# The upper parts of the last three output weights, rounded on GpSimd

## The chip, the cores and the metric

The kernel runs on one core of a Trainium2 chip. The metric is the device time of one execution in microseconds (us); three runs of the kernel before gave 1349.77, 1352.42 and 1352.82, median 1352.42. A matmul, the elementwise engines (VectorE is DVE in the profile, ScalarE is ACT, GpSimd is POOL) and the DMA queue of SyncE (SP) run side by side and wait for one another through semaphores.

## The reference

Two layers of cross attention run one after the other. Layer 0 works per batch with an attention over channels and a normalization; layer 1 is an ordinary attention with low-rank additions to its four weights:

```python
q = _lora_linear(hidden_states, Wq, Aq, Bq)      # 32 batches, 128 tokens, 1024 channels
k = _lora_linear(traces, Wk, Ak, Bk)             # 8 key heads, each for 4 query heads
v = _lora_linear(traces, Wv, Av, Bv)
scores = jnp.einsum('bhqd,bhtd->bhqt', q, k) / jnp.sqrt(jnp.asarray(HD, q.dtype))
attn = jax.nn.softmax(scores, axis=-1)
context = jnp.einsum('bhqt,bhtd->bhqd', attn, v)
out = _lora_linear(context, Wo, Ao, Bo)          # x @ Wo + 2 * (x @ Ao @ Bo)
return hidden_states + out
```

## The kernel before

All matmuls take float32 operands that are split in two: an upper part rounded to the matmul's format (fp32r), and a lower part, the float32 value less the upper part. Three matmuls (upper by upper, upper by lower, lower by upper) make one product.

Layer 0 with the key and value projections of layer 1 fills the first 415 us or so. Then one list of slots `w` sets the order of everything. Each engine's program walks through the same slots and issues its own share of each. Slots 0 to 255 (`QUERY_SLOTS = 256`) hold the query projection (`project_q`, L669), 8 slots to a pair of blocks; after them come 16 steps of 16 slots (`STEP`), one step for each pair of batches, with the output projection (`project_o`, L711). The other work of the attention is spread over the slots of both: scores (L730, with `maxima` on DVE, L1231 and L1236, and `exponents` on ACT, L981), scores a second time for the probabilities (`scores_again`, L763, one per slot, with `probabilities` on ACT, L998), and the context (L774, evacuated by ACT, L1011). `scores_again` of a slot alternates between two banks, so it waits until ACT has made the probabilities of the slot two before. The context of slots 2, 6, 10 and 14 of a step waits for them too.

The output projection of a pair of batches is a 2 by 2 product of blocks by seven products (Winograd's form of Strassen). Each product m has a combination of blocks of the context (`combine`, L1299 to L1314), split on DVE (`split_op`, L1289 upper, L1291 lower), and a combination of blocks of the weight, which is made once. GpSimd makes the three sums and one difference of weight blocks (`out_weights`, L1511, 16 instructions), the upper parts of all seven weights are rounded by ACT (`out_hi`, L891, two pieces of 128 by 1024 for each), and DVE takes the lower parts (`out_lo`, L1267, two pieces each). The tables `WO_UPPER` and `WO_LOWER` give the slot of each piece, counted from slot 256. Products 0 to 3 have theirs ahead of slot 256; those of products 4, 5 and 6 fall into slots 1 to 11 of the first step, beside its other work. The product m of the first step begins in slot 0, 2, 4, 7, 9, 11 or 13 of the step and waits for both pieces of its lower part (`wo_lo`, L681). DVE adds the finished products up in `add_out` (L1320).

The semaphore `wo_hi` counts ACT's pieces in order; `wo_mix` counts GpSimd's sums; `q_mm` counts blocks of the query projection, 64 in all. The upper parts of weights 4, 5 and 6 are written over tiles that the query projection reads, so they wait for its end, `q_mm` at 64 (L890).

Of the kernel before, what the change touches and what calls it, by code (L numbers as in the profile page):

```python
# [8 lines left out]
ALU = mybir.AluOpType  # L9
# [5 lines left out]
DMA = 16  # L15


def xattn_two_layers(nc, x, ctx_4096, Wq0, bq0, Wk0, bk0, Wv0, bv0, Wo0, bo0, gn_w, gn_b,
# [5 lines left out]
    NC = HID // P  # L24
# [11 lines left out]
    NG = B // GB  # L36
    PAIRS = B // 2
    PRODUCTS = 7
# [7 lines left out]
    with ExitStack() as ctx:  # L46
# [132 lines left out]
        def tile_at(name, place, dtype=F32):  # L179
            at[0] = place  # L180
            return sb(name, [P, GROUP, BANK], dtype)
# [3 lines left out]
        wo_raw = {0: w_blk[0], 1: w_blk[3], 2: w_sum[2], 3: w_sum[3], 4: w_blk[1], 5: w_blk[2], 6: w_sum[6]}  # L185
        hi_place = [*(w_place + i * BLOCK for i in (0, 4, 5, 6, 7)), hT_place, hT_place + BLOCK]
        lo_place = [block_place[0], block_place[3], sum_place[2], sum_place[3], block_place[1], block_place[2], sum_place[6]]
        wo = [[tile_at(f"wo{m}_{part}", place[m], F32R) for part, place in enumerate((hi_place, lo_place))]
              for m in range(PRODUCTS)]
# [17 lines left out]
        def f32(ap):  # L207
            return ap.bitcast(F32)
# [17 lines left out]
            "score_keys0", "score_keys1", *(f"again_in{i}" for i in range(4)), "rows_in0", "rows_in1", "v_in0", "v_in1", "sc_mm", "max", "neg", "exp",  # L226
            "ln", "lse", "lse_mm", "lse_hi", "lse_lo", "lse_out0", "lse_out1", "lse_out2", "lse_out3",
            "st_mm", "st_exp", "pv_mm", "c", "comb", "op_hi", "op_lo", "o_mm", "kept", "o",
            "wo_in0", "wo_in1", "wo_in2", "wo_in3", "wo_hi", "wo_lo", "wo_mix",
            "h_blk0", "h_blk1", "h_blk2", "h_blk3", "out0", "out1", "out2", "out3")}  # L230


# [10 lines left out]
        def units_of(b):  # L243
            if b == 0:
                return ()
            if b < 3:
                return (FIRST_Q + b - 1,)
            return (FIRST_Q + 2, FIRST_Q + 3) if b == 3 else (FIRST_Q + b,)
# [182 lines left out]

        WO_LOADS = {QUERY_SLOTS + w: i for i, w in enumerate((-31, -28, -23, -18))}
        WO_UPPER = {}
        for m, halves in enumerate(((-24, -23), (-11, -10), (-7, -6), (-3, -2), (1, 3), (4, 5), (7, 8))):
            for half, w in enumerate(halves):
                WO_UPPER.setdefault(QUERY_SLOTS + w, []).append((m, half))
        WO_LOWER = {}
        for m, halves in enumerate(((-18, -17), (-8, -7), (-4, -3), (-1, -1), (6, 7), (8, 9), (10, 11))):
            for half, w in enumerate(halves):
                WO_LOWER.setdefault(QUERY_SLOTS + w, []).append((m, half))  # L440

# [413 lines left out]
        def scalar_program(act):  # L855
# [25 lines left out]
            def out_hi(m, half):  # L881

                of = slice(2 * half, 2 * half + 2)
                if half == 0:
                    if m in (0, 1, 5):
                        act.wait_ge(S[f"wo_in{(0, 3, 0, 0, 0, 2)[m]}"], DMA)
                    else:
                        act.wait_ge(S["wo_mix"], {2: 3, 3: 1, 4: 2, 6: 4}[m])

                    act.wait_ge(S["q_mm"], NC * (NG - 1) + (1, 5, 6, 7, 8, 8, 8)[m])  # L890
                act.copy(wo[m][0][:, of, :], wo_raw[m][:, of, :]).then_inc(S["wo_hi"], 1)  # L891

            def begin_gram(b):
# [190 lines left out]
        def vector_program(dve):  # L1084
# [175 lines left out]
            def out_lo(m, half):  # L1260

                of = slice(2 * half, 2 * half + 2)
                if half == 0:

                    dve.wait_ge(S["wo_mix"], (1, 4, 4, 3, 2, 3, 4)[m])
                    dve.wait_ge(S["wo_hi"], 2 * (m + 1))
                dve.tensor_tensor(wo[m][1][:, of, :], wo_raw[m][:, of, :], f32(wo[m][0][:, of, :]),  # L1267
                                  ALU.subtract).then_inc(S["wo_lo"], 1)

# [158 lines left out]
            for w in range(END + 1):  # L1428
# [20 lines left out]
                for part in WO_LOWER.get(w, ()):  # L1449
                    out_lo(*part)  # L1450
# [28 lines left out]
        def gpsimd_program(pool):  # L1479

            pool.memset(lora_b3["kv"][:], 0.0)
            pool.memset(lora_a3["kv"][:], 0.0).then_inc(S["const"], 1)
            pool.memset(ident[:], 0.0).then_inc(S["const"], 1)
            pool.memset(score_bias[:], 0.0).then_inc(S["const"], 1)
            pool.wait_ge(S["const"], CONST["ident_zero"])
            pool.affine_select(out=ident[:], in_=ident[:], compare_op=ALU.not_equal, fill=1.0, base=0,
                               pattern=[[-1, P]], channel_multiplier=1).then_inc(S["const"], 1)

            mask = score_bias[:].rearrange("p (b e) -> p b e", b=H0)
            pool.wait_ge(S["const"], CONST["mask_zero"])  # L1490
            pool.affine_select(out=mask, in_=mask, compare_op=ALU.is_ge, fill=OFF_BLOCK, base=0,
                               pattern=[[-D0, H0], [0, D0]], channel_multiplier=1).then_inc(S["const"], 1)
            pool.wait_ge(S["const"], CONST["above"])
            pool.affine_select(out=mask, in_=mask, compare_op=ALU.is_ge, fill=OFF_BLOCK, base=D0 - 1,
                               pattern=[[D0, H0], [0, D0]], channel_multiplier=-1).then_inc(S["const"], 1)
            pool.memset(ones_row[:], 1.0).then_inc(S["const"], 1)
            pool.memset(minus_half[:], -0.5)
            pool.memset(ones_avg[:], 1.0 / P).then_inc(S["const"], 1)
            for m in ("q", "o"):
                pool.memset(lora_b3[m][:], 0.0)  # L1500
                pool.memset(lora_a3[m][:], 0.0).then_inc(S["const"], 1)

            def prep_rest(n):
                raw, hi, lo = prep_parts(n)
                pool.wait_ge(S["prep_hi"], n + 1)
                pool.tensor_tensor(lo, raw, f32(hi), ALU.subtract).then_inc(S["wkv_lo_pool" if n < FIRST_Q else "prep_lo"], 1)

            def out_sum(made, a, b):

                for c in range(GROUP):  # L1510
                    done = pool.tensor_tensor(made[:, c, :], a[:, c, :], b[:, c, :], ALU.subtract)  # L1511
                done.then_inc(S["wo_mix"], 1)

            def out_weights():
                b11, b12, b22, b21 = w_blk
                used = NC * (NG - 1)

                for i in range(2):
                    pool.wait_ge(S[f"wo_in{i}"], DMA)
                pool.wait_ge(S["q_mm"], used + 2)  # L1520
                out_sum(w_sum[3], b12, b11)
                pool.wait_ge(S["wo_in2"], DMA)
                pool.wait_ge(S["wo_mix"], 1)
                out_sum(b12, b22, b12)
                pool.wait_ge(S["q_mm"], used + 3)
                out_sum(w_sum[2], b22, w_sum[3])
                pool.wait_ge(S["wo_in3"], DMA)
                pool.wait_ge(S["q_mm"], used + 4)
                pool.wait_ge(S["wo_mix"], 3)
                out_sum(w_sum[6], b21, w_sum[2])  # L1530

            def power(b):
                pool.wait_ge(S["ve"], b + 1)
                pool.tensor_tensor(rstd, ve, minus_half[:], ALU.pow).then_inc(S["pow"], 1)

            def stack_lora(m):
                stack = S[f"lora_stack_{m}"]
                pool.wait_ge(S["const"], CONST[f"zero_{m}"])
                pool.wait_ge(S[f"lora_in_{m}"], LORA_IN[m])
                for q in range(3):  # L1540
                    pool.tensor_scalar(lora_a3[m][:, :, 32 * q:32 * q + R], lora_a[m][:, :, 0:R], 1.0, None,
                                       ALU.mult).then_inc(stack, 1)
                pool.tensor_scalar(lora_b[m][:], lora_b3[m][:], 1.0, None, ALU.mult).then_inc(stack, 1)
                pool.wait_ge(stack, 4)
                pool.tensor_tensor(lora_b[m][64:96, :], lora_b3[m][64:96, :], f32(lora_b[m][64:96, :]),
                                   ALU.subtract).then_inc(stack, 1)
                pool.wait_ge(stack, 5)

            for n in range(0, NC, 2):
                prep_rest(n)  # L1550
            for b in range(B):
                pool.wait_ge(S["x_hi"], b + 1)
                pool.tensor_tensor(x_lo[:], x_in[b % 2][:], f32(x_hi[:]), ALU.subtract).then_inc(S["x_lo"], 1)  # L1553
                if b and units_of(b - 1) and units_of(b - 1)[-1] < FIRST_O:
                    prep_rest(units_of(b - 1)[-1])
                if b:
                    power(b - 1)
                if b < 2:
                    stack_lora("qo"[b])
                for n in units_of(b)[:-1]:  # L1560
                    prep_rest(n)
            power(B - 1)

            pool.wait_ge(S["prep_mm"], N_UNITS)
            pool.wait_ge(S["h"], B)
            pool.memset(k_stack[LSE_ROWS, :, :, :].bitcast(F32), -1.0).then_inc(S["stack_ones"], 1)
            pool.wait_ge(S["stack_ones"], 1)
            out_weights()

        def sync_program(sp):  # L1570
# [342 lines left out]
```

## Time and profile before

| | |
|---|---|
| median of three runs | 1352.42 us |
| profiled execution | 1352.2 us |
| its span | 1350.4 us |
| granted clock of TensorE | 0.997 of full speed |
| busy PE, DVE, ACT, POOL | 98%, 69%, 61%, 12% of the span |

The profile's times are from the start of the span. Outside the span lie 1.8 us of the profiled execution. "Idle before" in a row is the time that the engine stood still ahead of that instruction, and behind the arrow stands what ended it. Step 0, the first pair of batches, runs on PE from 880.7 to about 915 us. POOL is idle from 863.4 us to the end.

### The profile page before, as it was taken

What the parts mean: (1) busy time and instruction counts of PE and PEld (TensorE: products, weight loads), DVE (VectorE), ACT (ScalarE), POOL (GpSimd) and SP (SyncE); (2) the same over time, 40 slices, a digit from 0 to 9 for tenths busy, and PEclk for the clock granted to TensorE, in tenths of its full rate; (3) what the DMA queues carried; (4) which work ended last, traced back from release to release, by engine and by line L of the source; (5) the groups of instructions that cost most, each with busy time, mean ns of one, the idle gap of its engine ahead of it and who ended that gap; (6) DMA issues with size and microseconds to landing.
All of it is one profiled execution on the core that took longest, in us unless ns stands there. A gap on an engine that the chain in (4) does not pass through costs nothing.

```text
span 1350.4 us, 23739 instructions
## 1 busy us (share of the span) xinstructions
PE 1326.5 (98%) x7135; PEld 1051.9 (78%) x7135; DVE 929.8 (69%) x2075; ACT 827.7 (61%) x2931; POOL 160.7 (12%) x129
## 2 busy tenths in 40 slices
PE   6999999999999999999999999999999999999999
PEld 4778888888888888888888888766767676766666
DVE  5666666666665777777777776586776777666666
ACT  4566666555550777777757776766566666665441
POOL 6533333222210000000000001400000000000000
PEclk9999999999999999999999999999999999999999
DMA  6455556667756888788777888989998999988872
GB/s 186 149 187 196 195 193 197 223 222 223 233 177 195 247 236 232 216 234 231 229 212 218 236 230 266 278 243 246 262 247 235 256 249 254 252 235 230 235 226 87
DMA packets 194817, 300.42 MB, mean 222 GB/s; under 512 B 26562, under 2 KB 93732, under 8 KB 194180
## 3 DMA queue, kind: packets, MB, share of 16 engines
q1 hardware_dynamic: 194692, 298.90, 76.6%
q8 instruction: 60, 0.98, 0.3%
q14 instruction: 65, 0.53, 0.1%
HBM read 213.88 MB, written 84.93 MB: 221 GB/s over the span
## 4 chain that ended last, share of the span: by engine, by line
PE 94%; DVE 2%; DMA 1%; ACT 1%; SPq 1%; issue 1%; DVEq 0%; ACTq 0%
PE bank L669 25%; PE bank L711 23%; PE bank L562 13%; PE bank L730 7%; PE bank L763 5%; PE bank L774 5%; PE bank L622 3%; PE bank L544 2%; PE bank L507 2%; PE bank L640 2%; PE bank L587 1%; PE bank L655 1%; PE bank L592 1%; PE bank L524 1%; PE bank L604 1%
## 5 line engine op out<-in xcount | busy, mean ns | idle before, releaser
L981 ACT ACTIVATE bank<-bank,negs 128x128 f32<-128x128 f32 x1024 | 347.2, 339 | 188.1 <-DVE negs L1236 187.7
L669 PE MATMUL bank<-hT,wq 128*128 128x512 f32 x1488 | 390.4, 400 | 0.0
L711 PE MATMUL bank<-wo,op 128*128 128x512 f32 x1344 | 345.7, 394 | 1.2 <-issue 1.2
L669 PEld LDWEIGHTS bank<-hT,wq 128*128 128x128 f32 x1488 | 263.9, 189 | 46.1
L711 PEld LDWEIGHTS bank<-wo,op 128*128 128x128 f32 x1344 | 249.0, 188 | 53.0 <-issue 2.4
L1231 DVE TENSOR_REDUCE maxes<-bank 128x4 f32<-128x512 f32 x256 | 175.5, 685 | 117.3 <-PE bank L730 116.9
L998 ACT ACTIVATE probT<-bank 128x512 f32<-128x512 f32 x256 | 151.2, 602 | 103.9 <-PE bank L763 101.4
L981 ACT ACTIVATION_READ_ACCUMULATOR bank<-bank,negs 128x1 f32 x1024 | 208.4, 204 | 0.0
L562 PE MATMUL bank<-wkv_hi,yT 128*128 128x512 f32 x512 | 201.5, 421 | 0.0
L730 PEld LDWEIGHTS bank<-k_stack,q_stack 96*128 96x128 f32 x1024 | 150.4, 191 | 16.3 <-issue 0.6
L730 PE MATMUL bank<-k_stack,q_stack 96*128 96x128 f32 x1024 | 147.3, 266 | 0.4 <-DMA q_stack<-q_dram 0.4
L763 PE MATMUL bank<-q_stack,k_stack 98*128 98x512 f32 x256 | 108.8, 426 | 1.7 <-ACT probT L998 1.7
L562 PEld LDWEIGHTS bank<-wkv_hi,yT 128*128 128x128 f32 x512 | 97.6, 191 | 13.8
L1553 POOL TENSOR_TENSOR x_lo<-x_in,x_hi 128x1024 fp32r<-128x1024 f32 x32 | 76.4, 2388 | 225.0 <-ACT x_hi L910 225.0
L562 PE MATMUL bank<-wkv_lo,yT 128*128 128x512 f32 x256 | 100.7, 393 | 0.0
L763 PEld LDWEIGHTS bank<-q_stack,k_stack 98*128 98x128 f32 x256 | 47.9, 187 | 66.9 <-issue 36.1
L1320 DVE TENSOR_TENSOR h_blk<-bank,h_blk 128x512 f32<-128x512 f32 x80 | 53.6, 686 | 66.5 <-PE bank L711 66.5
L868 ACT CAST yT<-bank 128x512 fp32r<-128x512 f32 x64 | 37.0, 580 | 94.2 <-PE bank L507 94.2
L1291 DVE TENSOR_TENSOR op<-c_sb,op 128x512 fp32r<-128x512 f32 x96 | 67.4, 702 | 3.3
L774 PE MATMUL bank<-probT,v_in 128*32 128x512 f32 x512 | 68.2, 604 | 1.1 <-ACT probT L998 1.0
L1236 DVE TENSOR_SCALAR negs<-maxes 128x4 f32<-128x4 f32 x256 | 44.9, 175 | 27.0
L1096 DVE TENSOR_TENSOR yT<-bank,yT 128x512 fp32r<-128x512 f32 x64 | 43.8, 685 | 24.9 <-ACT yT L868 24.9
(167 smaller groups left out, 1634.6 us busy)
## 6 DMA issues: line engine op xcount, KB each, us to landing
q_stack<-q_dram SPq DMA_DIRECT2D x256, 256.0 KB, 4.0
q_dram<-q_part SPq DMA_DIRECT2D x64, 512.0 KB, 4.2
q_stack<-q_dram SPq DMA_DIRECT2D x256, 128.0 KB, 4.3
y_in<-in_ctx SPq DMA_DIRECT2D x32, 512.0 KB, 4.4
x_in<-in_x SPq DMA_DIRECT2D x32, 512.0 KB, 5.2
h_dram<-h_out SPq DMA_DIRECT2D x32, 512.0 KB, 2.6
h_in<-h_dram SPq DMA_DIRECT2D x32, 512.0 KB, 3.7
k_stack<-k_dram SPq DMA_DIRECT2D x128, 128.0 KB, 3.4
```

What stands on the lines that cost most here:

```text
L562: m = pe.matmul(bank(2), yT[b % 2][:, c, part, :], w[:, c, :], start=first, stop=c == NC - 1 and part == 1)
L669: m = pe.matmul(bank(u % 2).rearrange("p (a n) -> p a n", a=2), wq[:, block, part, c, :], hT[(group + 1) % 2][:, :, of, c, :], start=c == ...
L711: mm = pe.matmul(out_bank(pair, m), op[m][:, of, c, :], wo[m][w][:, c, :], start=c == 0 and of == 0 and w == 0, stop=c == GROUP - 1 and of ...
L730: m = pe.matmul(score_bank(n)[:, j * P:(j + 1) * P], q_stack[place // GQ][SCORE_ROWS, g, j, :], k_stack[SCORE_ROWS, k % 2, g, :], start=Tr ...
L763: pe.matmul(again_bank(n), k_stack[STACK_ROWS, 2 + k % 2, g, :], again_stack(k)[STACK_ROWS, g, :, :].rearrange("p j n -> p (j n)"), start= ...
L774: m = pe.matmul(bank(3)[g * HD:(g + 1) * HD, :], v_in[:, k % 2, g, :], probT[:, (GQ * k + g) % PROBS, :], start=True, stop=True)
L981: act.activation(part, part, ACT.Exp, bias=negs[:, n % RING, j:j + 1], scale=SCORE1, accum_out=sums[:, score_column(k), g, j:j + 1]).then_ ...
L998: act.activation(probT[:, n % PROBS, :], again_bank(n), ACT.Exp, scale=SCORE1).then_inc(S["st_exp"], 1)
L1231: dve.tensor_reduce(largest, score_bank(n).rearrange("p (j t) -> p j t", j=GROUP), AX_X, ALU.max).then_inc(S["max"], 1)
L1291: dve.tensor_tensor(op_part(m, 1), tile, f32(op_part(m, 0)), ALU.subtract).then_inc(S["op_lo"], 1)
L1320: dve.tensor_tensor(block[:], *terms, ALU.add).then_inc(S["o"], 1)
L1553: pool.tensor_tensor(x_lo[:], x_in[b % 2][:], f32(x_hi[:]), ALU.subtract).then_inc(S["x_lo"], 1)
```

## The change

ACT no longer rounds the upper parts of weights 4, 5 and 6. GpSimd does, in six instructions behind its differences of blocks, once `q_mm` stands at 64; they count on a semaphore of their own, `wo_hi_pool`. The lower parts of the three weights stay on DVE, and their slots move: weight 4 from slots 6 and 7 to 4 and 5, weight 5 from 8 and 9 to 7 and 8, weight 6 from 10 and 11 to 9 and 10.

```diff
-        for m, halves in enumerate(((-24, -23), (-11, -10), (-7, -6), (-3, -2), (1, 3), (4, 5), (7, 8))):
+        for m, halves in enumerate(((-24, -23), (-11, -10), (-7, -6), (-3, -2))):
             for half, w in enumerate(halves):
                 WO_UPPER.setdefault(QUERY_SLOTS + w, []).append((m, half))
         WO_LOWER = {}
-        for m, halves in enumerate(((-18, -17), (-8, -7), (-4, -3), (-1, -1), (6, 7), (8, 9), (10, 11))):
+        for m, halves in enumerate(((-18, -17), (-8, -7), (-4, -3), (-1, -1), (4, 5), (7, 8), (9, 10))):
...
-                    dve.wait_ge(S["wo_hi"], 2 * (m + 1))
+                    dve.wait_ge(S["wo_hi"] if m < 4 else S["wo_hi_pool"], 2 * (m % 4 + 1))
...
                 out_sum(w_sum[6], b21, w_sum[2])
+
+                pool.wait_ge(S["q_mm"], NC * NG)
+                pool.wait_ge(S["wo_mix"], 4)
+                for m in range(4, PRODUCTS):
+                    for half in range(2):
+                        of = slice(2 * half, 2 * half + 2)
+                        pool.tensor_scalar(wo[m][0][:, of, :], wo_raw[m][:, of, :], 1.0, None,
+                                           ALU.mult).then_inc(S["wo_hi_pool"], 1)
```

GpSimd's queue at its end, behind the sums of blocks (`w_sum`, `w_blk`); `wo_0_142`, `wo_0_144` and `wo_0_146` are the upper parts of weights 4, 5 and 6:

```order
 L1511 TENSOR_TENSOR w_sum_131<-w_blk_128,w_blk_127 128x512 x4
 L1511 TENSOR_TENSOR w_blk_128<-w_blk_129,w_blk_128 128x512 x4
 L1511 TENSOR_TENSOR w_sum_132<-w_blk_129,w_sum_131 128x512 x4
 L1511 TENSOR_TENSOR w_sum_133<-w_blk_130,w_sum_132 128x512 x4
-L1868 UNCONDITIONAL_BRANCH
+L1537 TENSOR_SCALAR wo_0_142<-w_blk_128 128x1024 x2
+L1537 TENSOR_SCALAR wo_0_144<-w_blk_129 128x1024 x2
+L1537 TENSOR_SCALAR wo_0_146<-w_sum_133 128x1024 x2
```

The six new instructions are the last of that engine's program.

DVE in slots 5 to 9 of step 0; `wo_1_143`, `wo_1_145` and `wo_1_147` are the lower parts of weights 4, 5 and 6, `op_118` a part of the context's split, `maxes` and `negs` the maxima of the scores:

```order
+L1267 TENSOR_TENSOR wo_1_143<-w_blk_128,wo_0_142 128x1024
 L1289 TENSOR_SCALAR op_118<-c_sb 128x512
 L1291 TENSOR_TENSOR op_118<-c_sb,op_118 128x512
-L1267 TENSOR_TENSOR wo_1_143<-w_blk_128,wo_0_142 128x1024
 L1320 TENSOR_TENSOR s_sb<-bank,c_sb 128x512
 L1320 TENSOR_TENSOR h_blk_154<-s_sb,h_blk_154 128x512
 L1231 TENSOR_REDUCE maxes<-bank 128x4
 L1236 TENSOR_SCALAR negs<-maxes 128x4
-L1267 TENSOR_TENSOR wo_1_143<-w_blk_128,wo_0_142 128x1024
 L1267 TENSOR_TENSOR wo_1_145<-w_blk_129,wo_0_144 128x1024 x2
+L1267 TENSOR_TENSOR wo_1_147<-w_sum_133,wo_0_146 128x1024
 L1320 TENSOR_TENSOR h_blk_157<-bank,h_blk_157 128x512
```

Both pieces of weight 4 now stand ahead of the maxima of slot 7, and the first piece of weight 6 stands ahead of the maxima of slot 10. The number of DVE's instructions is the same.

ACT in slots 1 to 8 of step 0, the part of its queue that loses six roundings (`CAST`), as it stands before:

```order
L891 CAST wo_0_142<-w_blk_128 128x1024
L981 ACTIVATE bank,sums<-bank,negs 128x128 x4
L998 ACTIVATE probT<-bank 128x512
L1017 COPY c_sb<-bank 128x512
L998 ACTIVATE probT<-bank 128x512
L1011 COPY c_sb<-bank 128x512
L891 CAST wo_0_142<-w_blk_128 128x1024
L998 ACTIVATE probT<-bank 128x512
L891 CAST wo_0_144<-w_blk_129 128x1024
L998 ACTIVATE probT<-bank 128x512
L891 CAST wo_0_144<-w_blk_129 128x1024
```

In the changed kernel the same rows follow one another without the `CAST` rows.

## Rows read from the trace of the kernel before

**Rows 1.** Windows: busy us of PE, PEld, DVE, ACT, POOL; clock, DMA share, GB/s.

```profile
880.00:913.00 33.00, 29.63 (x148) 20.18 (x146) 30.71 (x49) 22.94 (x69) 0.00 (x0) 1.00 0.87 243
913.00:1340.00 427.00, 426.29 (x2101) 298.88 (x2098) 290.15 (x525) 239.73 (x683) 0.00 (x0) 1.00 0.87 235
```

**Rows 2.** Timeline of PE, step 0: start us, us long, instruction [idle before <- releaser].

```profile
889.34 0.51 PE L763 MATMUL bank<-q_stack,k_stack 98*128 98x512 f32 x1 [0.63 <-ACT probT L998]
...
893.80 0.51 PE L763 MATMUL bank<-q_stack,k_stack 98*128 98x512 f32 x1 [0.52 <-ACT probT L998]
...
895.33 1.06 PE L774 MATMUL bank<-probT,v_in 128*32 128x512 f32 x8 [1.02 <-ACT probT L998]
...
901.72 1.62 PE L711 MATMUL bank<-wo,op 128*128 128x512 f32 x6 [1.19 <-issue]
...
909.67 0.40 PE L763 MATMUL bank<-q_stack,k_stack 98*128 98x512 f32 x1
```

**Rows 3.** Timeline of ACT, step 0.

```profile
892.20 1.05 ACT L891 CAST wo<-w_blk 128x1024 fp32r<-128x1024 f32 x1
893.15 0.59 ACT L998 ACTIVATE probT<-bank 128x512 f32<-128x512 f32 x1
...
907.06 0.34 ACT L981 ACTIVATE bank<-bank,negs 128x128 f32<-128x128 f32 x1 [2.62 <-DVE negs L1236]
908.45 0.61 ACT L998 ACTIVATE probT<-bank 128x512 f32<-128x512 f32 x1
```

**Rows 4.** Timeline of DVE, end of the query projection and step 0.

```profile
882.39 0.68 DVE L1218 TENSOR_SCALAR q_part<-bank 128x512 fp32r<-128x512 f32 x1
...
889.89 0.69 DVE L1320 TENSOR_TENSOR h_blk<-c_sb,h_blk 128x512 f32<-128x512 f32 x1 [0.85 <-ACT c_sb L1017]
...
900.40 3.49 DVE L1267 TENSOR_TENSOR wo<-w_blk,wo 128x1024 fp32r<-128x1024 f32 x3
...
906.06 0.68 DVE L1231 TENSOR_REDUCE maxes<-bank 128x4 f32<-128x512 f32 x1
...
914.97 0.69 DVE L1320 TENSOR_TENSOR h_blk<-bank,h_blk 128x512 f32<-128x512 f32 x1 [2.15 <-PE bank L711]
```

**Rows 5.** Timeline of POOL, part of its sums of blocks.

```profile
852.63 5.02 POOL L1511 TENSOR_TENSOR w_sum<-w_blk,w_sum 128x512 f32<-128x512 f32 x4
...
857.82 5.60 POOL L1511 TENSOR_TENSOR w_sum<-w_blk,w_sum 128x512 f32<-128x512 f32 x4 [0.17 <-POOL w_sum L1511]
859.19 4.23 POOL L1511 TENSOR_TENSOR w_sum<-w_blk,w_sum 128x512 f32<-128x512 f32 x3
```

**Rows 6.** Timeline of DVE beside them.

```profile
855.27 1.15 DVE L1236 TENSOR_SCALAR negs<-maxes 128x4 f32<-128x4 f32 x1
...
858.11 1.67 DVE L1291 TENSOR_TENSOR op<-c_sb,op 128x512 fp32r<-128x512 f32 x1
```

**Rows 7.** Timeline of POOL, its two earlier roundings of 128 by 1024.

```profile
28.15 2.77 POOL L1543 TENSOR_SCALAR lora_b_q<-lora_b_q 128x1024 fp32r<-128x1024 f32 x1
...
41.47 2.78 POOL L1543 TENSOR_SCALAR lora_b_o<-lora_b_o 128x1024 fp32r<-128x1024 f32 x1
```

**Rows 8.** Timeline of DVE beside these two.

```profile
28.11 1.16 DVE L1174 TENSOR_SCALAR att<-att,att_stat 128x128 f32<-128x128 f32 x1
29.19 0.68 DVE L1096 TENSOR_TENSOR yT<-bank,yT 128x512 fp32r<-128x512 f32 x1
...
42.25 0.35 DVE L1174 TENSOR_SCALAR att<-att,att_stat 128x128 f32<-128x128 f32 x1
```

**Rows 9.** Groups by line: duration ns min/median/max; the last one busy us, mean ns, idle.

```profile
L1174 DVE TENSOR_SCALAR att<-att,att_stat x32: 285/287/1161, 28.1 to 391.4; 128x128 f32<-128x128 f32 x32
...
L1236 DVE TENSOR_SCALAR negs<-maxes x256: 169/170/1151, 438.7 to 1213.0; 128x4 f32<-128x4 f32 x128
...
L1267 DVE TENSOR_TENSOR wo<-w_blk,wo x8: 1212/1218/1226, 843.5 to 902.7; 128x1024 fp32r<-128x1024 f32 x8
...
L1291 DVE TENSOR_TENSOR op<-c_sb,op 128x512 fp32r<-128x512 f32 x96 | 67.4, 702 | 3.3
```

More of the change, by code:

```diff
@@ L228, in xattn_two_layers @@
             "st_mm", "st_exp", "pv_mm", "c", "comb", "op_hi", "op_lo", "o_mm", "kept", "o",
-            "wo_in0", "wo_in1", "wo_in2", "wo_in3", "wo_hi", "wo_lo", "wo_mix",
+            "wo_in0", "wo_in1", "wo_in2", "wo_in3", "wo_hi", "wo_hi_pool", "wo_lo", "wo_mix",
             "h_blk0", "h_blk1", "h_blk2", "h_blk3", "out0", "out1", "out2", "out3")}
@@ L884, in out_hi @@
                 if half == 0:
-                    if m in (0, 1, 5):
-                        act.wait_ge(S[f"wo_in{(0, 3, 0, 0, 0, 2)[m]}"], DMA)
-                    else:
-                        act.wait_ge(S["wo_mix"], {2: 3, 3: 1, 4: 2, 6: 4}[m])
-                    act.wait_ge(S["q_mm"], NC * (NG - 1) + (1, 5, 6, 7, 8, 8, 8)[m])
+                    if m < 2:
+                        act.wait_ge(S[f"wo_in{(0, 3)[m]}"], DMA)
+                    else:
+                        act.wait_ge(S["wo_mix"], {2: 3, 3: 1}[m])
+                    act.wait_ge(S["q_mm"], NC * (NG - 1) + (1, 5, 6, 7)[m])
                 act.copy(wo[m][0][:, of, :], wo_raw[m][:, of, :]).then_inc(S["wo_hi"], 1)
```

## The prediction

> **What bounds the kernel now.** I read the table of windows first, since the change touches one stage only. Behind step 0 PE has next to nothing to win: from 913 to 1340 us it stands still for 0.7 us, with DVE busy for 290 of 427 us [rows 1]. The stretch from 880 to 913 us is unlike it: PE is busy for 29.6 of 33 us, DVE for 30.7 [rows 1]. So in step 0 DVE sets the pace and PE follows it; behind it PE sets the pace, and whatever PE is late by at the end of step 0 is late by in the end, since no later idle time of PE can take it up.
>
> The reader should next see in PE's timeline where its 3.4 us of idle time are: 0.63, 0.52 and 1.02 us for probabilities from ACT, and 1.19 us ahead of product 4 [rows 2]. That last one has no releaser in the profile; DVE's three lower pieces began at 900.40 and the first of them, the second of weight 4, was done about 1.2 us later, at 901.6, just ahead of PE's start at 901.72 [rows 2, 4]. So it is the weight. ACT's timeline shows one cause of the others: a rounding of 1.05 us stood at 892.20 ahead of probabilities that PE wanted, done at 893.74 for PE's start at 893.80 [rows 2, 3]. At the far end of step 0 the probabilities of slot 10 (908.45 + 0.61 = 909.06) are ready 0.6 us before the scores of slot 12 begin at 909.67 [rows 2, 3]: that is PE's slack against DVE there, because the exponents ahead of them wait for DVE again, for 2.62 us [rows 3].
>
> **What goes from ACT.** Six roundings of 1.05 us, 6.3 us [rows 3]. ACT is busy for 22.9 of 33 us there [rows 1] and mostly waits for DVE, so only those ahead of wanted probabilities count: PE could win 0.52 + 1.02, and with the earlier lower part of weight 4 another 1.19, together 2.7 us, if nothing else held it. It does not keep them. After the roundings are gone the probabilities of slot 5 still stand behind the exponents of slot 5, and these behind DVE's maxima. I take this gain as passed on to the next wait for DVE, so at 0, and carry the 2.7 as a bound.
>
> **What moves on DVE.** It has the same instructions, without a pause between them in this stretch but for 0.85 us at 889 [rows 4]. A lower piece takes 1.14 us from one start to the next ((3.49 - 1.22) / 2, for three in a row with 1.22 as the length of the last [rows 4, 9]). Four pieces stood ahead of the maxima of slot 10 at 906.06 [rows 4], now five do. The maxima come 1.1 us later, and so do exponents and probabilities of slot 10; less PE's slack of 0.6 us that is +0.5 us for PE. The maxima of slots 5 and 7 are late by the same 1.1 us, but behind them PE has the room of the waits that go (2.7 us). All pieces are done by the maxima of slot 13 as before, so the order costs nothing further.
>
> **What comes to POOL.** Six instructions of the form of L1543, 2.77 us each [rows 7], 16.6 us from the end of the query projection at 880.7. The two pieces of weight 4 are there at about 887, those of weight 5 by 893 and of weight 6 by 899 even with some waiting; DVE asks for them at 893, 901 and 903 or later. So DVE never waits for the semaphore. It costs nothing as long as POOL isn't held up by more than some 4 us.
>
> **What POOL's instructions do to DVE's.** This is the term that decides. In the sums of blocks a DVE instruction that reads two SBUF tiles, or a rounding or scaling from SBUF to SBUF, stands until POOL's running instruction ends. The four of 852.63 take 1.25 us each, so one ends at 856.4: DVE's negation, 0.17 us long by itself [rows 9], began at 855.27 and lasted 1.15, to 856.42. POOL's of 857.82 ends at 859.1 (the next is recorded at 859.19): DVE's lower part, 0.70 by itself [rows 9], began at 858.11 and lasted 1.67, to 859.78 [rows 5, 6]. A subtraction with one operand from PSUM passed beside POOL's rounding in 0.68 us (L1096 at 29.19 [rows 8]). In step 0 nearly all of DVE's work is of the kind that stands still.
>
> What a rounding of 128 by 1024 on POOL holds, two instances show. L1174 takes 0.287 us, and once 1.16, once 0.35 [rows 8, 9]. The first ended at 29.27, so it began in truth at 28.98, 0.83 us behind POOL's start at 28.15. The second ended at 42.60, so at 42.31, 0.84 us behind POOL's start at 41.47. In both POOL lasted for 2.77 or 2.78 us [rows 7, 8]. I read this as: POOL's rounding keeps such DVE work out for its first 0.84 us and not for all of its 2.77. The bounds for one of them are 0 us (as the second, which lost 0.06) and 2.77 us (if it holds as the sums do).
>
> Six times 0.84 would be 5.0 us. Laid along DVE's queue from 880.7, with POOL starting as soon as its last is done and DVE's running instruction is over, the six starts meet: the second lower piece of weight 3, with the seam between two instructions (0.87 us lost), the first combination (0.25, since the two roundings of `q_part` from PSUM at 882.39 [rows 4] cover the rest), then the lower part of product 2 (0.82), the upper of 3 (0.87), the upper of 4 (0.87) and the lower of 5 (0.76): 4.4 us. About 0.2 of it goes into DVE's idle 0.85 ahead of 889.89 [rows 4].
>
> The sum for PE: 4.4 - 0.2 for the holds, + 1.1 for the order, - 0.6 for the slack = +4.7 us. The profiled execution took 1352.2 us, so 1356.9; it lay 0.2 below the median of the runs, so 1357.1 us. If POOL's rounding also keeps DVE's roundings out while it writes, it is up to 0.7 us more by the same laying out; with a second hold of 0.84 us in every piece against all kinds, 4 to 5 more, 1362.
>
> The Trainium skill ("SBUF — State Buffer", section "Who interferes with whom") says that a DVE instruction in a 2-port mode and GpSimd lock each other out, and that "whoever issues first gets the shared pair for the whole instruction". The sums of blocks agree; L1174 at 42.25 does not, for it was through 1.65 us before POOL's rounding ended. By the rule the result would be that of the first rival.
>
> **The rivals.** *The whole instruction is held.* For it speaks that the sums hold to their end [rows 5, 6]; against it the second L1174 [rows 8], though one short instruction is thin evidence. Six pieces of 2.77 are 16.6 us, less 2.1 in which DVE has three PSUM reads to do (0.7 each, as L1218 and L1231 in [rows 4]) and less 0.7 at the seams: 13.8 us lost, + 1.1 - 0.6 = +14.3, or 1366.7 us.
>
> *Nothing is held that matters* (not slower). POOL's rounding reads one tile, and no row shows DVE's two-input subtraction beside one; most of step 0's work may pass. Then the order remains, +0.5 us, 1352.9. Against it stands the first L1174.
>
> *ACT's relief decides* (not slower). Where DVE is not held and its new order doesn't reach PE, PE keeps the waits that go, 0.52 + 1.02 + 1.19 = 2.7 us [rows 2]: 1349.7. It decides only if the maxima of slots 5, 7 and 10 come no more than 0.6 us later than before. DVE's dense queue speaks against it. Even this whole gain is 0.2%.
>
> **Chances.** A partial hold 0.60, nothing held 0.20, all held 0.15, relief 0.05. Within 0.3%, which is what a measurement of this kernel can tell from no change, lies 1348.4 to 1356.5 us. The partial hold, itself 1354 to 1362, is above that in about 7 of 10 cases. So slower by over 0.3%: 0.42 + 0.15 = 0.57; within: 0.18 + 0.20 + 0.02 = 0.40; faster: 0.03. The range from 1351.8 to 1362 us takes in the partial hold and the case without any, and leaves out the full hold and the relief.
>
> **What would show it.** In the changed kernel's profile: six POOL roundings of 2.8 to 3.5 us from 880.7 or 881.3; six DVE instructions in step 0 drawn out to some 0.8 us more than their kind, each ending a fixed 0.84 us behind a start of POOL plus its own length; busy DVE from 880 to 913 near 33 us; no wait of PE ahead of product 4 by the weight; DVE's wait for product 6, which ends at 914.97 [rows 4], ending at about 919.7; the stretches behind it as before. If the drawn-out ones reach 2.5 us and end where POOL's end, the first rival is right; if none is drawn out, the second. A wait of DVE at L1267 for POOL would show my pace of POOL wrong.

## The result, and the profile after

The changed kernel takes 1355.7 us (median of 8 runs, 1354.72 to 1357.05) against 1352.05 us for the kernel before (8 runs): 1.003 times as long, 95% interval 1.002 to 1.004. The prediction was 1357.1 us, and slower by over 0.3% the likeliest case. The median lies 3.65 us above, 0.27%, so just inside the band around no change; the interval, 2.7 to 5.4 us, does not settle on which side of 0.3% the change lies. The profiled execution took 1354.72 us.

A finer measure than the time is the length of step 0 in the profile, from the start of its first output product to the start of the last half of product 6. Before it was 880.66 to 913.39, 32.7 us. Windows of the changed kernel, columns as in [rows 1]:

```profile
864.00:877.00 13.00, 13.00 (x68) 8.98 (x67) 7.70 (x12) 10.53 (x28) 0.00 (x0) 1.00 0.99 275
878.00:916.00 38.00, 31.47 (x149) 21.28 (x148) 34.42 (x48) 18.40 (x67) 17.68 (x6) 0.96 0.78 215
917.00:1340.00 423.00, 422.29 (x2081) 295.45 (x2080) 287.97 (x521) 238.08 (x676) 0.00 (x0) 1.00 0.89 236
```

Ahead of step 0 and behind it PE stands still for 0.7 us in all, as in [rows 1]; within it, for 6.5 of 38. The timeline of PE there:

```profile
878.08 1.54 PE L711 MATMUL bank<-wo,op 128*128 128x512 f32 x6
...
889.13 0.50 PE L763 MATMUL bank<-q_stack,k_stack 98*128 98x512 f32 x1 [3.02 <-ACT probT L998]
889.47 2.69 PE L711 MATMUL bank<-wo,op 128*128 128x512 f32 x6
...
896.94 1.61 PE L711 MATMUL bank<-wo,op 128*128 128x512 f32 x6 [0.24 <-DVE h_blk L1320]
900.82 0.50 PE L763 MATMUL bank<-q_stack,k_stack 98*128 98x512 f32 x1 [2.27 <-ACT probT L998]
...
905.31 0.50 PE L763 MATMUL bank<-q_stack,k_stack 98*128 98x512 f32 x1 [1.00 <-ACT probT L998]
...
911.91 0.46 PE L763 MATMUL bank<-q_stack,k_stack 98*128 98x512 f32 x1
...
915.71 1.55 PE L711 MATMUL bank<-wo,op 128*128 128x512 f32 x6
```

Step 0 lasts from 878.08 to 915.71, 37.6 us: 4.9 us more. The waits of [rows 2] are other ones now: 0.63 has become 3.02, the pair in slots 5 and 6 is gone, 2.27 and 1.00 stand in slots 7 and 9, and nothing waits ahead of product 4. That this step began 2.6 us earlier than before is no gain of the change: over the thirteen profiles of this study it began between 877.4 and 881.1 us, and two executions of the changed kernel differ in it by 1.6 us.

The timeline of DVE after, the rows that are longer than their kind, with some of their neighbours (compare [rows 4] and [rows 9]):

```profile
877.52 3.20 DVE L1267 TENSOR_TENSOR wo<-w_sum,wo 128x1024 fp32r<-128x1024 f32 x2
...
881.97 0.97 DVE L1299 TENSOR_TENSOR c_sb<-c_sb 128x512 f32<-128x512 f32 x1
...
883.77 0.64 DVE L1289 TENSOR_SCALAR op<-s_sb 128x512 fp32r<-128x512 f32 x1
884.44 1.40 DVE L1291 TENSOR_TENSOR op<-s_sb,op 128x512 fp32r<-128x512 f32 x1
...
886.55 0.50 DVE L1236 TENSOR_SCALAR negs<-maxes 128x4 f32<-128x4 f32 x1
886.63 0.68 DVE L1310 TENSOR_TENSOR c_sb<-c_sb 128x512 f32<-128x512 f32 x1
887.35 1.14 DVE L1289 TENSOR_SCALAR op<-c_sb 128x512 fp32r<-128x512 f32 x1
...
889.97 1.52 DVE L1320 TENSOR_TENSOR h_blk<-c_sb,h_blk 128x512 f32<-128x512 f32 x1 [0.75 <-ACT c_sb L1017]
...
893.19 1.14 DVE L1289 TENSOR_SCALAR op<-c_sb 128x512 fp32r<-128x512 f32 x1
```

And of POOL:

```profile
878.10 11.85 POOL L1537 TENSOR_SCALAR wo<-w_blk 128x1024 fp32r<-128x1024 f32 x4 [16.71 <-PE bank L669]
889.91 5.87 POOL L1537 TENSOR_SCALAR wo<-w_sum 128x1024 fp32r<-128x1024 f32 x2
```

The six roundings take 2.8 to 3.3 us each and are done at 895.8, before DVE asks for the last of them at 905.4. The DVE rows, each less the length of its kind before (2.36, 0.68, 0.43, 0.69, 0.43, 0.69, 0.43), exceed it by 0.84, 0.29, 0.21, 0.71, 0.71, 0.83 and 0.71: 4.3 us. The negation at 886.55 is 0.33 longer, but the next instruction began at once and is not, so that costs nothing.

### The profile page after: what moved, and what is told of

The parts are those of the page before. It is cut to its first block, busy times and chain, and to the rows that moved or that the text cites. A ratio compares the mean times of both kernels' runs of the same rounds, so it can differ in the third digit from the quotient of the medians.

```text
span 1352.8 us, 23737 instructions
## 1 busy us (share of the span) xinstructions
PE 1326.9 (98%) x7135; PEld 1051.6 (78%) x7135; DVE 933.6 (69%) x2075; ACT 823.2 (61%) x2925; POOL 178.3 (13%) x135
## 4 chain that ended last, share of the span: by engine, by line
PE 94%; DVE 3%; ACT 1%; issue 1%; DMA 1%; SPq 0%; DVEq 0%; ACTq 0%
PE bank L669 25%; PE bank L711 22%; PE bank L562 13%; PE bank L730 7%; PE bank L763 5%; PE bank L774 5%; PE bank L622 3%; PE bank L507 2%; PE bank L544 2%; PE bank L640 2%; PE bank L587 1%; PE bank L655 1%; PE bank L592 1%; PE bank L524 1%; PE bank L604 1%
## 5 line engine op out<-in xcount | busy, mean ns | idle before, releaser
L711 PE MATMUL bank<-wo,op 128*128 128x512 f32 x1344 | 346.5, 395 | 0.2 <-DVE h_blk L1320 0.2
L711 PEld LDWEIGHTS bank<-wo,op 128*128 128x128 f32 x1344 | 249.7, 189 | 51.8 <-issue 1.2
L763 PE MATMUL bank<-q_stack,k_stack 98*128 98x512 f32 x256 | 109.2, 428 | 6.9 <-ACT probT L998 6.9
L763 PEld LDWEIGHTS bank<-q_stack,k_stack 98*128 98x128 f32 x256 | 48.1, 188 | 73.2 <-issue 38.8
L1511 POOL TENSOR_TENSOR w_sum<-w_blk,w_blk 128x512 f32<-128x512 f32 x4 | 5.0, 1292 | 425.5 <-DMA w_blk<-wo_dram 425.5
```

Source lines behind the costliest of these rows:

```text
L711: mm = pe.matmul(out_bank(pair, m), op[m][:, of, c, :], wo[m][w][:, c, :], start=c == 0 and of == 0 and w == 0, stop=c == GROUP - 1 and of ...
L763: pe.matmul(again_bank(n), k_stack[STACK_ROWS, 2 + k % 2, g, :], again_stack(k)[STACK_ROWS, g, :, :].rearrange("p j n -> p (j n)"), start= ...
```

## The experiments

"Step 0" is the measure above, 32.7 us in the kernel before and 37.6 in the changed one. The ratios are to the kernel before, on the same chip.

**The new order alone.** The kernel before with

```diff
-(-1, -1), (6, 7), (8, 9), (10, 11))):
+(-1, -1), (4, 5), (7, 8), (9, 10))):
```

> The kernel before with only the lower pieces moved to their new slots; the upper parts stay on ScalarE. Theory (GpSimd's roundings hold VectorE up for 0.84 us each, and the new order costs a little): from the first product of step 0 to its last (32.7 us before, 37.6 us in the changed kernel) it takes 33.2 to 34.4 us, and the whole kernel 0.5 to 1.7 us more than before. Rival (the new order is the cause of the loss): 36 us or more, and 3.5 us more in all. Rival (ScalarE's relief is what counts, the order helps): shorter than 32.7 us.

Step 0 took 34.3 us (879.82 to 914.11), 1.6 more; the time was 1.0017 of before, 1.0008 to 1.0027. The order is not the cause of the loss, though it is a part of it. In PE's timeline the waits of slots 3, 5 and 6 stay word for word, the 1.19 ahead of product 4 is gone, and three take its place further on:

```profile
898.36 0.50 PE L763 MATMUL bank<-q_stack,k_stack 98*128 98x512 f32 x1 [0.54 <-ACT probT L998]
902.85 0.50 PE L763 MATMUL bank<-q_stack,k_stack 98*128 98x512 f32 x1 [1.02 <-ACT probT L998]
910.27 0.50 PE L763 MATMUL bank<-q_stack,k_stack 98*128 98x512 f32 x1 [0.66 <-ACT probT L998]
```

They are the maxima that stand behind the earlier lower pieces. This run holds more than the order, though: with ScalarE still rounding, DVE now asked for weight 6 before ScalarE had it, and stood still for 0.76 us, ahead of the maxima of slot 10:

```profile
903.84 1.23 DVE L1267 TENSOR_TENSOR wo<-w_sum,wo 128x1024 fp32r<-128x1024 f32 x1 [0.76 <-ACT wo L891]
```

The changed kernel has no such wait. So 1.6 us is too much for the order by itself; the next two runs give it without ScalarE's roundings.

**GpSimd's roundings alone.** The changed kernel with the old `WO_LOWER`.

> The changed kernel with the lower pieces in their old slots: GpSimd rounds, nothing else moves. Theory of the hold: step 0 takes 36.5 to 37.3 us (4.3 us of held VectorE work less at most 0.5 us of slack), the kernel some 4 us more than before; VectorE shows the same six drawn-out instructions. Rival (the new order is the cause): about 32.7 us, no change.

Step 0 took 37.0 us (880.35 to 917.37), 4.3 more; the time was 1.0031 of before, 1.0019 to 1.0042. The loss is there without the new order. GpSimd's roundings alone bring 4.3 of the 4.9 us, the order 0.6 on top.

**No roundings at all.** The six `pool.tensor_scalar` of the changed kernel taken out, and

```diff
+        for m in range(4, PRODUCTS):
+            wo[m][0] = wo[m - 3][0]
```

> The changed kernel, new order, with the six roundings of GpSimd left out: products 4, 5 and 6 use the upper parts of weights 1, 2 and 3, so this part of the result is another one. ScalarE has its relief, GpSimd nothing to do in step 0. Theory of the hold: step 0 takes 33.2 to 33.8 us (0.5 to 0.9 over before, from the order), no wait of TensorE over 1.5 us, and no fall of its clock. Rival (nothing is held, the loss is the order with ScalarE's queue): still about 37 us. Rival (the relief of ScalarE is worth 2.7 us): about 30 us.

Step 0 took 33.65 us, 0.9 more than before and 4.0 less than the changed kernel. The time was 1.0012 of before (1.0002 to 1.0022). No DVE instruction in it is drawn out. So the order costs 0.9 us without ScalarE's roundings, and GpSimd's roundings 4.0 us. One thing expected did not hold: TensorE waited for over 2 us once, and its clock did fall. Some 0.3 of the 0.9 us can be put down to that fall, by an estimate: the probabilities of slot 10 were ready at 909.13, and PE began the scores of slot 12 at 909.56, 0.43 us later, where in the changed kernel it was 0.08 (911.83 and 911.91). That leaves 0.6 for the order, as in the comparison above.

**The old order without the late roundings.**

> The kernel before with the six late roundings of ScalarE left out and nothing in their place: products 4 to 6 use the upper parts of weights 1 to 3, so this part of the result is another one. Theory (VectorE sets the pace of step 0, ScalarE's relief is passed on to the next wait): step 0 takes 32.5 to 33.0 us, as before, with the waits of 0.52 and 1.02 us for probabilities in slots 5 and 6 gone and new ones of the same sum in slots 7 to 9. Rival (the relief is worth what these waits are): 30 to 31.3 us.

Step 0 took 32.75 us, the same as before to 0.02; the time was 1.0005 (0.9994 to 1.0016). PE's timeline (line numbers are two higher, L765 is the old L763, L713 the old L711):

```profile
888.61 0.50 PE L765 MATMUL bank<-q_stack,k_stack 98*128 98x512 f32 x1 [0.64 <-ACT probT L1000]
897.33 0.50 PE L765 MATMUL bank<-q_stack,k_stack 98*128 98x512 f32 x1 [1.31 <-ACT probT L1000]
901.01 1.63 PE L713 MATMUL bank<-wo,op 128*128 128x512 f32 x6 [1.54 <-issue]
```

The 0.52 and 1.02 us of slots 5 and 6 are gone, and 1.31 in slot 7 and 0.35 more ahead of product 4 have come: 1.54 given up, 1.66 taken. In the old order relieving ScalarE is worth nothing. In the new order it is worth 0.6 us (34.3 against 33.65), for there DVE's wait of 0.76 us for ScalarE goes with it. That wait came with the new order, so it is no gain over the kernel before.

**Roundings timed to harmless work.** The changed kernel, old order, each rounding behind a wait of its own for a count that DVE reaches:

```diff
+                pace = iter((("wo_lo", 8), ("op_lo", 3), ("op_lo", 4), ("op_lo", 6), ("wo_lo", 9), ("wo_lo", 12)))
```

> The changed kernel with the lower pieces in their old slots, and each of GpSimd's six roundings waits for the VectorE instruction ahead of one that reads PSUM or of an idle time, so that its first 0.84 us fall beside work that can't be held. Theory (only the first 0.84 us are held): step 0 takes 33.2 to 34.2 us, and the six held instructions lose under 1.2 us together. Rival (a rounding holds for all of its 2.8 us): 42 us or more. Rival (a hold at its start and one at its end while it writes, each 0.84 us against all of VectorE's work): 35 us or more.

DVE's held work was 1.1 us in all (0.28, 0.17, 0.45 and 0.24), as expected: the same six instructions on GpSimd, at other moments, cost DVE a quarter. That excludes a hold of 2.8 us. Yet step 0 took 35.5 us, more than any figure of the theory; the rival with two full holds, 35 us or more, has the figure, but not the rows, which show 1.1 us held in all. The median of twelve executions was 1352.44 us (1.001 of before, 1.000 to 1.002). The profiled one was the longest, 1357.2 us, and not by step 0 alone: far behind it PE waited once for a DMA, which has nothing to do with the roundings:

```profile
1194.94 0.47 PE L763 MATMUL bank<-q_stack,k_stack 98*128 98x512 f32 x1 [1.61 <-DMA q_stack<-lse_dram]
```

Windows of step 0 in which PE was late:

```profile
904.00:906.00 2.00, 2.00 (x9) 1.64 (x8) 2.00 (x3) 1.19 (x4) 0.35 (x1) 0.63 0.86 220
906.00:908.00 2.00, 2.00 (x7) 1.71 (x7) 1.97 (x5) 0.43 (x1) 2.00 (x1) 0.51 0.69 190
908.00:909.00 1.00, 1.00 (x7) 0.35 (x10) 0.89 (x3) 0.26 (x1) 0.42 (x1) 1.00 0.80 252
```

The granted clock, the third value from the end, was at 0.5 of full speed (the 1.2 GHz level) for some 3.4 us. PE had stood still for 1.75 us ahead of 899.48 and for 1.81 ahead of 903.40.

> The paced kernel once more, for a second profile. In the first, step 0 took 35.5 us against 33.2 to 34.2 expected, with VectorE's held work at the 1.2 us expected and TensorE's clock below full from 904 to 910 us. Theory (the excess is the clock, which fell after two idle times of TensorE of 1.8 us): with the same fall step 0 takes 35.5 us again, without it 33.3 to 34.0. Rival (the excess is VectorE or ScalarE): 35.5 us also where the clock stays full.

The second profile: step 0 took 33.95 us, with the clock down again, but from 898 to about 901, right behind an idle time of 1.77 us:

```profile
898.00:899.00 1.00, 1.00 (x4) 0.82 (x3) 0.87 (x2) 0.45 (x1) 1.00 (x1) 0.50 0.79 176
899.00:901.00 2.00, 2.00 (x5) 1.02 (x4) 1.89 (x4) 0.41 (x3) 1.53 (x1) 0.50 0.94 269
```

In this one PE then still waited 0.43 us for the weight ahead of product 4, so the slow stretch was over before PE was the late one. The theory as it was put is half wrong: the clock fell and the time was short all the same. PE's rows from the start of product 4 to that of product 5, in the first profile and in the second, show where the 1.6 us between them lie:

```profile
903.40 1.91 PE L711 MATMUL bank<-wo,op 128*128 128x512 f32 x6 [1.81 <-issue]
...
909.93 1.54 PE L711 MATMUL bank<-wo,op 128*128 128x512 f32 x6
```

```profile
901.45 1.63 PE L711 MATMUL bank<-wo,op 128*128 128x512 f32 x6 [0.43 <-issue]
...
906.41 1.55 PE L711 MATMUL bank<-wo,op 128*128 128x512 f32 x6
```

This stretch took 6.53 us in the first, with the clock down and no wait in it, and 4.96 in the second, at full clock. What stands ahead of it in step 0 took 22.28 and 22.27 us, what stands behind it 6.70 and 6.72. So the whole 1.6 us are the clock's, in a stretch where PE waited for nobody. The fall costs nothing where PE would have waited for DVE next anyway, as in the second.

**Two inputs on GpSimd.**

```diff
-                        pool.tensor_scalar(wo[m][0][:, of, :], wo_raw[m][:, of, :], 1.0, None,
-                                           ALU.mult).then_inc(S["wo_hi_pool"], 1)
+                        pool.tensor_tensor(wo[m][0][:, of, :], wo_raw[m][:, of, :], wo_raw[m][:, of, :],
+                                           ALU.add).then_inc(S["wo_hi_pool"], 1)
```

> The changed kernel with GpSimd making the upper parts of weights 4 to 6 by adding the tile to itself (two inputs) in place of scaling it by one, so these parts and what comes of them are doubled in part. Theory (a two-input instruction on GpSimd holds VectorE's work to its end, 2.4 us; the scaling does so for its first 0.84 us only): step 0 takes 44 to 46 us, the kernel some 12 us more than before, and VectorE's held instructions end where GpSimd's end. Rival (each GpSimd instruction costs VectorE the same 0.84 us whatever its form): 36 to 38 us.

Step 0 took 41.05 us (877.40 to 918.45), 8.3 more than before; the time was 1.0054 of before (1.0037 to 1.007). Each instruction is shorter on GpSimd, 2.38 us, and costs far more. DVE beside them:

```profile
876.84 4.06 DVE L1267 TENSOR_TENSOR wo<-w_sum,wo 128x1024 fp32r<-128x1024 f32 x2
...
883.31 2.20 DVE L1307 TENSOR_TENSOR s_sb<-c_sb 128x512 f32<-128x512 f32 x1
885.54 2.00 DVE L1289 TENSOR_SCALAR op<-s_sb 128x512 fp32r<-128x512 f32 x1
887.57 2.26 DVE L1291 TENSOR_TENSOR op<-s_sb,op 128x512 fp32r<-128x512 f32 x1
```

The rival of one price for every form of instruction is out. The figure of 44 to 46 was too high: it let GpSimd wait for the whole of each DVE instruction between two of its own, but GpSimd's first four took 9.85 us, 2.46 each, so it lost under 0.1 us to each, and all six were through after 14.2 us.

**Half the size.** Twelve roundings of 128 by 512 in place of six.

> The changed kernel with each of GpSimd's roundings in two of 128 by 512. Theory (the hold is the time in which the input is read, one column after another, so 0.42 us for 512): step 0 takes 35.5 to 37.5 us, as the changed kernel or a little less, with twelve short delays on VectorE. Rival (0.84 us for every instruction): 40 us or more. Rival (held to the end): 46 us or more.

Step 0 took 36.1 us (1.0019 of before, 1.0008 to 1.0029), 3.3 more. DVE shows delays of about 0.3 us (0.97 for a kind of 0.69, 0.71 for 0.43), at most 0.41, and 2.7 us in all, in place of 4.3. So the hold is not a fixed price of an instruction: with half the columns it is half as long or less.

**Both engines by themselves.** The kernel before with trials behind its end; in the first two

```diff
+                    last = pool.tensor_scalar(probT[:, 0:2, :], c_sb[:, 0:2, :], 1.0, None, ALU.mult)
```

> The kernel before with six trials behind its end, some 20 us more, that touch no result: in each GpSimd runs one instruction of 128 by 1024 (scaling in trials 1 and 2, a two-input subtraction in 3 and 4, a fill in 5 and 6) and VectorE beside it twelve instructions of 128 by 128, two-input ones in the odd trials and scalings from SBUF to SBUF in the even ones. Theory: beside GpSimd's scaling VectorE's two-input instructions stand still once, for its first 0.84 us, and pass freely after; its scalings stand still there and a second time of at most 0.9 us near the end, while GpSimd writes (as the 0.50 us of a negation at 902.0 in the paced kernel suggests); beside the subtraction both stand still until its end at 2.4 us; beside the fill only the scalings are held. Rival: the scaling holds in several stretches of 0.3 us or more over its 2.8 us, for two-input work too.

Timelines of POOL (all six trials: scaling, subtraction and fill, each beside two-input work of DVE and then beside its scalings) and of DVE (from trials 1 to 3):

```profile
1345.39 2.88 POOL L1597 TENSOR_SCALAR probT<-c_sb 128x1024 f32<-128x1024 f32 x1 [484.82 <-DVE wo L1490]
1348.72 3.13 POOL L1597 TENSOR_SCALAR probT<-c_sb 128x1024 f32<-128x1024 f32 x1 [0.45 <-DVE wo L1495]
1352.36 2.34 POOL L1599 TENSOR_TENSOR probT<-c_sb 128x1024 f32<-128x1024 f32 x1 [0.51 <-DVE wo L1490]
1356.88 3.61 POOL L1599 TENSOR_TENSOR probT<-c_sb 128x1024 f32<-128x1024 f32 x1 [2.18 <-DVE wo L1495]
1360.97 0.96 POOL L1601 MEMSET probT<- 128x1024 f32 x1 [0.48 <-DVE wo L1490]
1363.33 2.32 POOL L1601 MEMSET probT<- 128x1024 f32 x1 [1.40 <-DVE wo L1495]
```

```profile
1345.55 1.12 DVE L1488 TENSOR_TENSOR wo<-wo,wo 128x128 fp32r<-128x128 f32 x1
1346.60 0.28 DVE L1490 TENSOR_TENSOR wo<-wo,wo 128x128 fp32r<-128x128 f32 x1
...
1348.82 1.06 DVE L1493 TENSOR_SCALAR wo<-wo 128x128 fp32r<-128x128 f32 x1
1349.80 0.21 DVE L1495 TENSOR_SCALAR wo<-wo 128x128 fp32r<-128x128 f32 x1
...
1352.41 2.44 DVE L1490 TENSOR_TENSOR wo<-wo,wo 128x128 fp32r<-128x128 f32 x1
```

Beside the scaling at 1345.39 one two-input instruction stood still and ended at 1346.67, so it began at 1346.39, 1.0 us behind POOL's start; the eight behind it passed in 0.28 us each while POOL worked on until 1348.27. A DVE scaling beside the next one did the same (begun in truth at 1349.67, 0.95 behind POOL's start), and those behind it passed. Beside the two-input subtraction at 1352.36 DVE's instruction ended at 1354.85, just behind POOL's end at 1354.70. Beside the subtraction at 1356.88 and beside the fill at 1363.33 DVE's scalings were not held, at 0.21 and 0.22 us each; GpSimd's instruction was, 3.61 us in place of 2.34 and 2.32 in place of 0.96: the opposite of what was expected of both. Beside the fill at 1360.97 DVE's two-input instructions went on at 0.28 us. The Trainium skill ("SBUF — State Buffer", section "Who interferes with whom") lets two SBUF inputs of DVE contend only with a GpSimd instruction that reads SBUF: by that fill, the trials agree. By its lock for a whole instruction the scaling would have held DVE for 2.9 us; the trials disagree, with 1.0. The end of POOL's scaling had no DVE scaling beside it in the trial, so the second hold wasn't tried there; that it exists rests on two rows of the changed kernel. The negation of 0.50 us at 886.55 ended at 887.05; less its own 0.17 it began in truth at 886.88, 0.15 us ahead of the end of POOL's third rounding at 887.03. The rounding of 0.64 us at 883.77, less its own 0.43, began in truth at 883.98, again 0.15 ahead of the end of POOL's second at 884.13.

**A better order for the kernel before.** Three additions and two splits of DVE stand later in step 0, behind maxima and lower pieces:

```diff
+                    sums_at = ({6: (3,), 7: (4,), 10: (5, 6), 11: (7, 8, 9), 13: (10,)} if pair == 0 else
+                               {6: (3, 4), 9: (5, 6), 11: (7, 8, 9), 13: (10,)})
...
-                    if i == 5:
+                    if i == (8 if pair == 0 else 5):
                         split_op(pair + 1, 0)
-                    if i == 9:
+                    if i == (11 if pair == 0 else 9):
                         split_op(pair + 1, 1)
```

> The kernel before with four of VectorE's works of step 0 (one sum, two additions to blocks, two splits for the next pair) moved behind the maxima and lower pieces that TensorE waits for; ScalarE rounds as before. Theory (VectorE's order sets step 0): step 0 takes 31.4 to 32.4 us, 0.3 to 1.2 less than before, and the wait of 1.19 us ahead of product 4 is gone; in the time of the kernel that is at most 0.1%. Rival (another engine sets the pace): 32.7 us.

Step 0 took 31.5 us, 1.2 less, and the wait of 1.19 is gone; the time was 0.9993 of before, 0.9984 to 1.0002, which can't be told from no change. Half of the 1.2 us is lost right behind the point at which the measure ends:

```profile
912.74 0.50 PE L763 MATMUL bank<-q_stack,k_stack 98*128 98x512 f32 x1 [0.33 <-ACT probT L998]
```

From the last half of product 6 (910.86) to the next product (913.08) it took 2.22 us, in the kernel before 1.61 (913.39 to 915.00); in the other runs it is 1.61 or 1.62. DVE's order sets step 0, but there is little to have.

**The changed kernel once more.**

> The changed kernel once more, for a second profile. Theory: step 0 takes 37.4 to 37.8 us again whatever the stretch ahead of it takes, and VectorE's six or seven drawn-out instructions are the same, with 4.1 to 4.5 us in all. Rival (chance of one execution): a step 0 of under 36 or over 39 us.

Step 0 took 37.6 us, from 879.66 to 917.28, and the seven rows of DVE are the same to 0.01 us. The 4.9 us are no chance of one execution.

## Why the prediction was right

*What bounds it.* DVE sets step 0's pace and what PE is late by stays. From step 0's start to the end of the span it was 469.7 us before and 474.7 and 474.7 in the two profiles after: 5.0 us, all of it step 0's 4.9.

*The hold.* 0.84 us for each rounding from two rows of another place in the kernel [rows 7, 8]; 4.4 us in all, measured 4.3. The held instructions began in truth 1.40, 0.90, 1.05, 1.06, 0.89 and 1.21 us behind POOL's recorded starts, so not at the fixed distance that was named as a sign. But POOL's roundings took 3.29, 2.77, 2.93, 2.94, 2.80 and 3.10 us, and with what each had above 2.77 taken off, which I read as its own wait for DVE's running instruction, the six are 0.86 to 0.90. The six starts met the work that I had laid out for four of them (lower piece of weight 3, first combination, lower part of product 2, upper of 3). The fifth and the sixth were a little off: the addition at 889.97 and the upper part of product 5. The six excesses add up to 4.1 us, 0.3 less than the laying out. The seventh, 0.21 us at 883.77, near the end of POOL's second rounding, is of the second hold that I had priced at 0 with up to 0.7 above it. So 4.3 against 4.4 is closer than the working was: one small miss made up for the other.

*Idle time taken up.* 0.2 expected, 0.1 measured: DVE's idle 0.85 became 0.75.

*The order.* + 1.1 us for the maxima of slot 10, less 0.6 of slack. These maxima began 30.75 us into step 0 after (908.83 less 878.08) and 25.40 before (906.06 less 880.66), 5.35 later: 4.2 for the hold and 1.1 for the order. PE's scores of slot 12 came 4.8 later, so the slack was 0.5. The + 0.5 for the order, the 1.1 less the slack, came out at 0.6 between the two orders with GpSimd's roundings. The sum 4.7 stands against 4.9 in the profile.

*The time.* 1352.2 + 4.7 + 0.2 = 1357.1 against 1355.7. The kernel before came out at 1352.05 in eight runs, and the ratio's interval holds both 4.7 and 4.9. The median rose by 3.65 us only, a quarter less than the 4.9 of the profiles; executions of one kernel differ by more than that. By the prediction's own bound of 1356.5 us the median lies in the band around no change, which had 0.40, and not in the one above it, which had 0.57. What was right is the mechanism, the partial hold, and its size in step 0.

*ScalarE's relief at 0.* Shown by the kernel without late roundings in the old order: step 0 differs by 0.02 us.

*The rivals.* A full hold is excluded by the kernel itself (step 0 would have been near 47 us), by the paced one and by the trials. No hold is excluded by taking the roundings out. The relief is excluded.

*What was not foreseen.* Right behind PE's 3.02 us of idle time its clock fell. Windows after:

```profile
889.00:890.00 1.00, 0.86 (x3) 0.73 (x4) 0.25 (x2) 0.83 (x3) 1.00 (x2) 0.77 0.84 227
890.00:891.00 1.00, 1.00 (x4) 0.80 (x3) 1.00 (x1) 0.34 (x1) 1.00 (x1) 0.50 0.10 33
891.00:892.00 1.00, 1.00 (x4) 0.71 (x4) 0.96 (x3) 0.00 (x0) 1.00 (x1) 0.50 0.51 129
892.00:893.00 1.00, 1.00 (x6) 0.90 (x5) 1.00 (x2) 0.37 (x1) 1.00 (x2) 0.52 0.97 352
893.00:896.00 3.00, 3.00 (x18) 1.60 (x18) 2.93 (x4) 1.21 (x3) 2.78 (x1) 1.00 0.51 132
```

A half product took 2.69 us at 889.47 in place of 1.55. By the rows it cost nothing in the end, since PE waited another 0.24, 2.27 and 1.00 us for DVE's chain behind it, and DVE's timeline has no idle time from 889.97 to 914.4, so DVE never waited for the slow PE. No run took the fall away by itself. In the first paced profile there were no such waits behind it, and step 0 grew by 1.6 us.

## What to carry to other kernels

An engine that looks idle can still hold up the one that sets the pace: before work is moved to GpSimd, look in the trace for VectorE instructions that are longer than their kind beside GpSimd's, separately for each form of instruction, since here a one-input rounding of 2.8 us held VectorE for 0.84 to 1.0 us and a two-input one of 2.4 us to its end. Relief for an engine that mostly waits for another is easily worth nothing; take the wait away on paper and see which wait comes next. Where a stretch is a few tens of microseconds of a long kernel, its length in the profile tells apart what the kernel's time cannot: 37.63 and 37.62 us in two executions of the changed kernel, whose times spread over 2.3 us. Even so look at the clock in each, for the paced kernel's two differ by 1.6 us, and look just behind the end of the measure, where the better order lost half of its gain.

## What the runs showed of the hardware

- GpSimd's scaling of 128 by 1024 (2.77 to 2.88 us) keeps out VectorE's two-input and SBUF-to-SBUF scaling work for about its first 0.84 to 1.0 us, and lets both pass in its middle. Near its end it held a short VectorE scaling or rounding until 0.15 us ahead of its own end; behind the negation so held, the next instruction with two inputs was not delayed.
- A two-input addition or subtraction of 128 by 1024 on GpSimd (2.34 to 2.38 us) held VectorE's two-input work to its end, 2.44 us in place of 0.28 in the trial, and in the kernel with two inputs a rounding too, 2.00 us in place of 0.43.
- A fill on GpSimd didn't hold VectorE's scalings, but was itself drawn out from 0.96 to 2.32 us by a dense row of them; a two-input subtraction waited in the same way behind VectorE's scalings, 3.61 us in place of 2.34.
- TensorE's granted clock fell to 0.5 in step 0 of nine of the thirteen profiles, for some 3.4 us in eight of them and nearly 7 us in the one with two inputs on GpSimd. In eight it came behind or, with two inputs, within idle times of 1.8 to 8.3 us. The ninth is the kernel with the trials, whose step 0 is that of the kernel before, after waits of no more than about 1 us; its step 0 took 32.9 us against 32.7 in the profile without a fall. Nor does every such idle time bring a fall: 2.27 and 2.25 us in the changed kernel's two profiles, 2.25 in the one with halves and 1.75 in the first paced one brought none right behind them.
